# A four-layer block on one core: three single-pass products on high and low parts for the gate and up products, a new order of the turn, and a quarter of a state product on VectorE

## The reference

```
w = spline_reconstruct(control_points)          # gate, up, down: [2048,512], [2048,512], [512,2048]
x = x + (silu(h @ gate.T) * (h @ up.T)) @ down.T       # h = layernorm(x)

dA = jnp.exp(d[..., None] * A)                   # for each step of 512, 512 channels, 16 states
state = state * dA + (d * u)[..., None] * b[:, None, :]
y = jnp.einsum('bdn,bn->bd', state, c)
```

## Time and profile before

| | |
|---|---|
| median of 3 runs | 1876.14 us |
| the profiled execution | 1873.21 us, its span 1871.4 us |
| granted TensorE clock, mean | 0.925 |
| TensorE busy | 1607.1 us (86%) |
| GpSimd busy | 1143.8 us (61%) |
| VectorE busy | 1109.2 us (59%) |
| ScalarE busy | 904.2 us (48%) |
| DMA | 276.31 MB, mean 148 GB/s |

### The profile page before, as it was taken

One profiled execution on the slowest core, in us unless ns is written; L12 is line 12 of the kernel. 1 busy time (PEld: TensorE's weight loads), 2 busy tenths in 40 slices (PEclk: granted clock), 3 DMA queues, 4 the chain that ended last, 5 costly groups with the idle time before them and its releaser, 6 DMA issues. The chain is left out here.

```text
span 1871.4 us, 25251 instructions
## 1 busy us (share of the span) xinstructions
PE 1607.1 (86%) x5972; PEld 993.6 (53%) x5973; DVE 1109.2 (59%) x2007; ACT 904.2 (48%) x1355; POOL 1143.8 (61%) x578
## 2 busy tenths in 40 slices
PE   4888847999999999999999546489999999999996
PEld 2333323444444444444444236368887887788885
DVE  3556675565656565656566555955656556556653
ACT  3344425455555555555555353734544445445442
POOL 0222135887878787878789211256666666667664
PEclk9878868999999999999999765589999999999998
DMA  3221044666767676667566753168888888888875
GB/s 124 79 80 66 15 167 129 165 149 126 171 149 149 126 171 149 149 126 170 128 142 124 190 169 137 39 152 197 187 194 187 194 190 183 194 200 194 193 146 105
DMA packets 88164, 276.31 MB, mean 148 GB/s; under 512 B 12321, under 2 KB 13250, under 8 KB 76338
## 3 DMA queue, kind: packets, MB, share of 16 engines
q0 software_dynamic: 42656, 150.93, 41.4%
q1 hardware_dynamic: 45458, 124.79, 21.5%
HBM read 148.78 MB, written 126.90 MB: 147 GB/s over the span
## 5 line engine op out<-in xcount | busy, mean ns | idle before, releaser
L694 DVE TENSOR_TENSOR_SCAN B_E<-bank,B_E 128x512 f32<-128x512 f32 x256 | 306.2, 1211 | 206.7 <-ACT bank L649 199.2
L737 POOL TENSOR_TENSOR B_E<-B_E,B_Cb 128x2048 f32<-128x2048 f32 x64 | 291.9, 4560 | 110.7 <-DVE B_E L694 110.7
L1572 POOL DMA_INDIRECT out_x<-D_y,D_rows x144 | 263.3, 1829 | 84.7 <-issue 43.7
L731 POOL TENSOR_TENSOR B_E<-B_dtu,B_Bb 128x2048 f32<-128x2048 f32 x64 | 292.2, 4567 | 32.9 <-DMA B_Bb<-bc_d 32.9
L610 PE MATMUL bank<-B_Wd,B_inter 128*128 128x512 f32 x512 | 230.7, 597 | 33.2 <-DVE X L688 32.4
L600 PE MATMUL bank<-hT,B_Wg 128*128 128x512 f32 x512 | 236.5, 606 | 23.6 <-DVE B_inter L683 22.5
L649 ACT ACTIVATE bank<-B_dtv,negA 128x512 f32<-128x512 f32 x256 | 171.8, 687 | 137.8 <-DVE B_E L694 137.0
L600 PE MATMUL bank<-hT,B_Wu 128*128 128x512 f32 x512 | 230.2, 592 | 0.0
L1537 POOL DMA_INDIRECT D_rows<-rows_d,D_source x144 | 150.1, 1042 | 127.6 <-DMA out_x<-D_y,D_rows 63.6
L1351 PE MATMUL bank<-W_gu_hi,D_xT_hi 128*128 x580 | 210.8, 363 | 1.0 <-ACT D_xT_hi L1410 0.9
L1352 PE MATMUL bank<-W_gu_lo,D_xT_hi 128*128 x580 | 196.6, 339 | 0.0
(11 more groups left out here) (270 smaller groups left out, 2821.5 us busy)
## 6 DMA issues: line engine op xcount, KB each, us to landing
y_d<-B_E POOLq DMA_DIRECT2D x64, 1024.0 KB, 8.1
W_raw_gu<-in_wgu SPq DMA_DIRECT2D x64, 384.0 KB, 4.7
B_Bb<-bc_d SPq DMA_DIRECT2D x32, 512.0 KB, 5.4
B_Cb<-bc_d SPq DMA_DIRECT2D x32, 512.0 KB, 3.8
W_raw_d<-in_wd SPq DMA_DIRECT2D x64, 256.0 KB, 4.4
rows_d<-C_row SPq DMA_DIRECT2D x4, 1090.0 KB, 4.8
X<-in_x SPq DMA_DIRECT2D x4, 1024.0 KB, 9.1
dt_d<-A_dtv SPq DMA_DIRECT2D x4, 1024.0 KB, 3.9
```

The source lines that it names most:

```text
L694: v.tensor_tensor_scan(E[:, s % NR, c, :], dA[m % 2][:, :], E[:, s % NR, c, :], 0.0, ALU.mult, ALU.add).then_inc(s_done, 1)
L731: g.tensor_tensor(E[:, s % NR, :, :], dtu[b % 2][:, :, :], spread(Bb[jj % 2][:, s % 2, :]), ALU.mult).then_inc(dbu_done, 1)
L737: g.tensor_tensor(E[:, s % NR, :, :], E[:, s % NR, :, :], spread(Cb[jj % 2][:, s % 2, :]), ALU.mult).then_inc(prod_done, 1)
L1572: g.indirect_dma_start(a["out"], bass.IndirectOffsetOnAxis(ap=rows[i][:, ROW - 1:ROW].bitcast(U32), axis=0), ysb[:, i, :], None, compute_o ...
```

## The change

**Products.** hT and the weights are kept as a high part (rounded to the single-pass format) and a low part (the rest). Every gate and up product becomes three single-pass ones: high by high, high by low, low by high. Tiles of hT get a second instruction on VectorE (`turn_lo`), weight units as well (`unit_lo`); of a gate or up unit the blend is now done in PSUM, before ScalarE's copy. Room for the low parts comes from single buffers for masks and drive input, three row buffers BC of one row each, inter chunks in three buffers with silu in place, and coefficients in DRAM (coef_d), of which one group at a time is loaded.

**Order.** In a turn `gate_up` of chunk 0 comes first, then a unit, the down products, a unit and `gate_up` of chunk 1. On ScalarE and VectorE decays, silus, scans and the rest are interleaved anew.

**Last quarter.** GpSimd's `weigh` covers three quarters and waits for three; VectorE's `weigh_last` does the fourth.

```diff
-            hT = s.enter_context(nc.sbuf_tensor("hT", [P, KC, NB * L], F32))
-            coef = s.enter_context(nc.sbuf_tensor("coef", [NSEL, 3, INTER], F32R))
+            hT_hi, hT_lo = (s.enter_context(nc.sbuf_tensor(f"hT_{h}", [P, KC, NB * L], F32R)) for h in ("hi", "lo"))
+            coef_gu = s.enter_context(nc.sbuf_tensor("coef_gu", [NSEL, 2, GW], F32R))
+            coef_dn = s.enter_context(nc.sbuf_tensor("coef_dn", [NSEL, D], F32R))
             powers = s.enter_context(nc.sbuf_tensor("powers", [NSEL, KC, 2, P], F32R))
...
+            sp.wait_ge(c_lo, 8)
+            sp.dma_start(coef_gu[:, :, :].bitcast(F32), coef[:, 0:2, 0:GW].bitcast(F32)).then_inc(coef_moved, 16)
+            sp.dma_start(coef_d[:, 0:2, :], coef[:, 0:2, :].bitcast(F32)).then_inc(coef_moved, 16)
+            sp.wait_ge(c_lo, 12)
+            sp.dma_start(coef_dn[:, :].bitcast(F32), coef[:, 2, 0:D].bitcast(F32)).then_inc(coef_moved, 16)
+            sp.dma_start(coef_d[:, 2, :], coef[:, 2, :].bitcast(F32)).then_inc(coef_moved, 16)
+            sp.wait_ge(coef_moved, 64)
...
+            def turn_lo(t):
+                v.wait_ge(hT_first, t + 1)
+                v.tensor_tensor(hT_lo[:, :, t * P:(t + 1) * P], bank[t % 2][:, :].rearrange("p (k l) -> p k l", k=KC),
+                                hT_hi[:, :, t * P:(t + 1) * P], ALU.subtract).then_inc(hT_done, 1)
...
                 v.tensor_scalar(xn[:, t % 2, :], X[:, t, :], mv[:, t, 0:1], rstd[:, t:t + 1], ALU.subtract, ALU.mult).then_inc(xn_done, 1)
+                if t >= 1:
+                    turn_lo(t - 1)
+            turn_lo(NT - 1)
...
-                act.activation(hT[:, :, t * P:(t + 1) * P], bank[t % 2][:, :].rearrange("p (k l) -> p k l", k=KC), ACT.Copy).then_inc(hT_done, 1)
-            act.wait_ge(ld_pw, 16)
+                act.activation(hT_hi[:, :, t * P:(t + 1) * P], bank[t % 2][:, :].rearrange("p (k l) -> p k l", k=KC), ACT.Copy).then_inc(hT_first, 1)
...
-        Wg, Wu = [sb(f"Wg{i}", [P, KC, GW]) for i in range(2)], [sb(f"Wu{i}", [P, KC, GW]) for i in range(2)]
+        Wg, Wu = ([[sb(f"W{n}_{h}{i}", [P, KC, GW], F32R) for h in ("hi", "lo")] for i in range(2)] for n in ("g", "u"))
-        words = [sb(f"masks{i}", [P, GW + D // 2], I32) for i in range(2)]
-        msk = [w[:, :].bitcast(U8) for w in words]
-        sil = [sb(f"sil{i}", [P, L]) for i in range(2)]
-        inter = [sb(f"inter{i}", [P, 2, L]) for i in range(2)]
-        dtv, dtu = sb("dtv", [P, KC, L]), [sb(f"dtu{i}", [P, KC, L]) for i in range(2)]
-        Bb, Cb = [sb(f"Bb{i}", [P, 2, L]) for i in range(2)], [sb(f"Cb{i}", [P, 2, L]) for i in range(2)]
-        NR = 4
+        words = sb("masks", [P, GW + D // 2], I32)
+        msk = words[:, :].bitcast(U8)
+        NI, NBC, NR = 3, 3, 4
+        inter = [sb(f"inter{i}", [P, L]) for i in range(NI)]
+        dtv, dtu = sb("dtv", [P, KC, L]), sb("dtu", [P, KC, L])
+        BC = [sb(f"BC{i}", [P, L]) for i in range(NBC)]
         E = sb("E", [P, NR, KC, L])
...
+        def drive_op(s):
+            return s if s < 2 else 2 * s - 1
+        def weigh_op(s):
+            return 2 * s + 2 if s + 2 < STEPS else STEPS + s
...
+            def op_done(op):
+                s, drives = steps[op]
+                sp.wait_ge(dbu_done if drives else prod_done, s + 1)
+                if not drives:
+                    sp.wait_ge(last_done, s + 1)
+            def load_row(op):
+                s, drives = steps[op]
+                if op >= NBC:
+                    op_done(op - NBC)
+                sp.dma_start(BC[op % NBC][:, :], spread(s % NS + (0 if drives else NS), s // NS)).then_inc(ld_bc[op % NBC], 16)
+            steps = {drive_op(s): (s, True) for s in range(STEPS)}
+            steps.update({weigh_op(s): (s, False) for s in range(STEPS)})
+            load_row(0)
             load_dtu(0)
             for c in range(KC):
                 load_dtv(0, c)
-            for b in range(NB):
-                for j in range(NJ):
-                    jj = NJ * b + j
-                    if jj >= 2:
-                        sp.wait_ge(dbu_done, 2 * (jj - 1))
-                    sp.dma_start(Bb[jj % 2][:, :, :].rearrange("p n l -> p (n l)"), spread(0, b, j)).then_inc(ld_b[jj % 2], 16)
...
+            load_masks(0)
+            for op in range(1, 2 * STEPS):
+                load_row(op)
+                s, drives = steps[op - NBC] if op >= NBC else (0, True)
+                b, group = (s + 1) // NS, s // 8 + 1
+                if drives and (s + 1) % NS == 0 and b < NB:
+                    load_dtu(b)
+                if not drives and (s + 2) % NS == 0 and s + 2 < STEPS:
+                    for c in range(KC):
+                        sp.wait_ge(dA_done, (s + 1) * KC + c + 1)
+                        load_dtv((s + 2) // NS, c)
+                if not drives and s % 8 == 0 and group < 2 * NB:
+                    units = NU if s == 0 else unit_job[(s // 2 - 1, 1)][0] + 1
+                    sp.wait_ge(used, units)
+                    sp.dma_start(coef_gu[:, :, :].bitcast(F32), coef_d[:, 0:2, group * GW:(group + 1) * GW]).then_inc(ld_coef, 16)
+                    if group % 2 == 0:
+                        sp.dma_start(coef_dn[:, :].bitcast(F32), coef_d[:, 2, group // 2 * D:(group // 2 + 1) * D]).then_inc(ld_coef, 16)
+                    load_masks(group)
...
-                        mm = pe.matmul(ps[:, :], W[:, k, ch * P:(ch + 1) * P], hT[:, k, tb * L:(tb + 1) * L], start=k == 0, stop=k == KC - 1)
+                        hi, lo = (t[:, k, ch * P:(ch + 1) * P] for t in W)
+                        h_hi, h_lo = (t[:, k, tb * L:(tb + 1) * L] for t in (hT_hi, hT_lo))
+                        pe.matmul(ps[:, :], hi, h_hi, start=k == 0, stop=False)
+                        pe.matmul(ps[:, :], hi, h_lo, start=False, stop=False)
+                        mm = pe.matmul(ps[:, :], lo, h_hi, start=False, stop=k == KC - 1)
...
+                gate_up(jj, 0)
                 if (jj, 0) in unit_job:
                     n, g = unit_job[(jj, 0)]
                     weights(n, unit_of(jj, 0), g)
-                gate_up(jj, 0)
+                if jj:
+                    down(jj - 1)
                 if (jj, 1) in unit_job:
                     n, g = unit_job[(jj, 1)]
                     weights(n, unit_of(jj, 1), g)
-                if jj:
-                    down(jj - 1)
                 gate_up(jj, 1)
...
-            def copy_unit(n, unit, buf):
-                act.wait_ge(a_ps, n + 1)
-                act.activation(w_unit(unit, buf), A_[n % 2][:, :], ACT.Copy).then_inc(a_used, 1)
+            def unit_first(n, unit, buf):
+                if unit < 4:
+                    act.wait_ge(blended, blends_ahead(n) + 1)
+                    act.activation(w_unit(unit, buf, 0), A_[n % 2][:, :], ACT.Copy).then_inc(first_done, 1)
+                else:
+                    act.wait_ge(a_ps, n + 1)
+                    act.activation(Wd[buf][:, unit - 4, :], A_[n % 2][:, :], ACT.Copy).then_inc(first_done, 1)
             def silu(jj, ch):
                 n = chunk_job[(jj, ch)]
                 act.wait_ge(a_ps, n + 1)
-                act.wait_ge(b_used, n - 1)
-                act.activation(sil[n % 2][:, :], A_[n % 2][:, :], ACT.Silu).then_inc(a_used, 1)
+                if 2 * jj + ch >= NI:
+                    act.wait_ge(y_ps, 4 * (jj - 1 + ch))
+                act.activation(chunk(jj, ch)[:, :], A_[n % 2][:, :], ACT.Silu).then_inc(sil_done, 1)
...
+            def unit_and_decay(jj, pos, s, c):
+                if (jj, pos) not in unit_job:
+                    decay(s, c)
+                    return
+                n, g = unit_job[(jj, pos)]
+                unit = unit_of(jj, pos)
+                if unit < 4:
+                    decay(s, c)
+                unit_first(n, unit, g % 2)
+                if unit >= 4:
+                    decay(s, c)
...
+            decay(0, 0)
+            decay(0, 1)
             for jj in range(NB * NJ):
-                for c in range(KC):
-                    decay(2 * jj, c)
-                if (jj, 0) in unit_job:
-                    n, g = unit_job[(jj, 0)]
-                    copy_unit(n, unit_of(jj, 0), g % 2)
+                decay(2 * jj, 2)
+                decay(2 * jj, 3)
                 silu(jj, 0)
-                if (jj, 1) in unit_job:
-                    n, g = unit_job[(jj, 1)]
-                    copy_unit(n, unit_of(jj, 1), g % 2)
-                for c in range(KC):
+                unit_and_decay(jj, 0, 2 * jj + 1, 0)
+                for c in range(1, KC):
                     decay(2 * jj + 1, c)
+                if jj < NB * NJ - 1:
+                    unit_and_decay(jj, 1, 2 * jj + 2, 0)
+                    decay(2 * jj + 2, 1)
                 silu(jj, 1)
...
-                v.wait_ge(a_used, n + 1)
+                m = msk[:, unit % 2 * 2 * GW:(unit % 2 + 1) * 2 * GW] if unit < 4 else msk[:, 4 * GW + (unit - 4) * D:4 * GW + (unit - 3) * D]
+                v.wait_ge(ld_msk, 16 * (g + 1))
```

(64 more changed lines are left out.)

118 lines of the change are left out of this document (58 added, 60 removed).

## The result

The changed kernel takes 1938.08 us (median of four runs, 1935.45 to 1941.49) where the kernel before takes 1875.12 (1872.77 to 1880.24): a ratio of 1.0333, with a 95% interval from 1.0306 to 1.036: slower by 63 us. The forecast was 1770, faster by 5.6%.

A forecast was written before the change was run, and what follows sets the result against it. A ring of waits in the feed-forward/state stage, paced by TensorE, the fullest engine, bounds the kernel. −141 + 11 + 9 + 6 + 7 + 4 = −104 us from 1873.2 gives 1769, stated as 1770; forecast 1745 to 1800 (0.58), wider range 1735 to 1840.

The forecast's parts named there:

- the hold: VectorE's last-quarter product waits only until the running GpSimd product ends; the other bound, none, saves 22 us in all.
- The rule that the forecast weighed: VectorE instruction with two SBUF inputs and GpSimd one reading SBUF exclude each other for a whole instruction; sum follows it.
- 583: First to last weighing: 21 turns of 18.9 us plus 10.5 of 17.7, against 724.1 before, −141 us.
- +11: GpSimd products beside which a held VectorE instruction slips in take longer: 63 × 0.17 us.
- +9: Batch changes: single-buffered drive input reloads, some 3 us stay, three times; bounds 3 and 15 us.
- +6 +7 +4: Before the first weighing: preparation's tiles +6, four coefficient moves +7 (bounds 3 and 12), new stage's start to first weighing +4.
- 18.3: TensorE's need per turn with units, in us, with single-pass products at 0.22; 17.4 without units.
- B: Rival, slower: even step's last quarter misses its window, held to W+7.9 (W: weighing's start), 23.4 us turns, 1912 us; chance 0.09.
- A: Rival, missed windows: odd step's last quarter late, held 4.5 us more; all 14 missing gives 1827 us; chance 0.20.
- C: Rival, no hold: VectorE's last-quarter product passes as the additions do, 1737 us; chance 0.10.
- D: Rival: single-pass gate and up products take as long as full-precision ones, 0.43 us each, over 1900 us; chance 0.01.
- The signs named ahead: Profile signs: 18.9 us turns, last-quarter product about 1.0 to 1.5 us; near 3 means A, turn over 22 B, 0.65 C.

The follow-up runs named there:

- The run with GpSimd's own wait: Changed kernel, register values masked, GpSimd's next drive waiting for the end of GpSimd's own weighing: 1816.48 us, ratio 0.9715.
- the control: Changed kernel with only three register values (expert numbers) masked in the last stage, an edit every further variant carries: 1945.28 us, ratio 1.038.
- the product from PSUM: Changed kernel, values masked, fourth scan written to PSUM so VectorE's last-quarter product reads one input there: 1780.03 us, ratio 0.952.
- The floor without the last quarter: Changed kernel, values masked, last quarter weighed by neither engine, GpSimd's transfer waiting for all four scans: 1764.54 us.
- the pair of runs that differ in the passes alone: Changed kernel, masked, last-quarter product from PSUM: single-pass gate and up products 1780.03 us, one full-precision product of the high parts 1849.33 us.
- the one-input operation: Changed kernel, masked, last-quarter product replaced by VectorE's tensor_scalar on one SBUF tensor and two scalars: 1987.35 us, unreadable as a total; stage 738.0 against 758.6.

## Why the prediction was wrong

**The step that failed is the hold.** The forecast took from four normalizations that "VectorE waited for the end of the running GpSimd instruction, then got in before or beside the following one", and wrote "I take the hold, until the running GpSimd product ends". It is so in 33 of 64 cases. In 16 the product arrived in time and was passed over, and in 12 it came after the weighing's end. Instead of about 1.0 to 1.5 us it lasts 4.12. The row that the forecast read the earlier trace rows was read rightly, and did not hold the case. Its 14.08 us are three held normalizations and one that was not (0.53 us), between these products of GpSimd and that of 261.39:

```profile
256.83 4.60 POOL L437 TENSOR_TENSOR B_Rgate<-B_Rgate,B_table 128x2048 f32<-128x2048 f32 x1 [18.35 <-DMA B_select<-in_select]
257.37 4.34 DVE L445 TENSOR_SCALAR B_xn<-X,B_mv,B_rstd 128x512 f32<-128x512 f32 x1 [0.30 <-PE bank L458]
261.64 4.72 DVE L445 TENSOR_SCALAR B_xn<-X,B_mv,B_rstd 128x512 f32<-128x512 f32 x1
266.04 4.68 POOL L437 TENSOR_TENSOR B_Rdown<-B_Rdown,B_table 128x2048 f32<-128x2048 f32 x1
266.28 4.72 DVE L445 TENSOR_SCALAR B_xn<-X,B_mv,B_rstd 128x512 f32<-128x512 f32 x1
```

Each held one ended 0.28 to 0.29 us after the product that ran, the first two with the next product directly behind. So VectorE was let in at every boundary there; but no product stood directly behind a transfer issue, as 26 of the 64 weighings of the changed kernel do. What failed is the step from three normalizations to 64 products beside another sequence of GpSimd instructions.

The run with GpSimd's own wait is the kernel with the forecast's hold, let in at the end of every weighing for which the product is in time. It has 628.8 us from first to last weighing against 758.6 of the control: the boundaries at which VectorE was passed over, or came late because of it, cost 130 us.

The rule that the forecast weighed (the Trainium skill, "SBUF — State Buffer", Who interferes with whom) says that whichever of the two comes first holds the other off for the whole instruction. That the two exclude each other agrees with the traces here, and it spoke against the change. How long the waiting one can stay shut out does not follow from it: here it was up to four instructions of GpSimd, and 12.4 us.

**The sum, term by term.** From first to last weighing the forecast had 583 + 11 + 9 = 603 us; measured are 758.2, 155 more. Some 130 of these are the missed boundaries. The other 26 are seen in the run with GpSimd's own wait: its turns without a reload take 19.3 us on average, where 583 + 11 over 31.5 turns is 18.9, and its three turns with a reload 26.3 to 26.4, so 21 us more for the three where **+9** was forecast, with a bound of 15. The mean of its held products is 2.4 us and not 1.0 to 1.5, so even a hold to the next boundary was priced too low. With the product from PSUM, which has no hold and no slip-in, the stage takes 594.1 us: 18.2 a turn, and 24.9, 25.2 and 26.1 for the three with a reload. The forecast without a hold had 22 us less than 583, 17.8 a turn, so the rest of the turn was about right. The **+11** for drives beside a slip-in came true in kind (4.96 to 5.08 us instead of the 4.5 of before where VectorE got in, about three times the 0.17 taken).
The start: **+6 +7 +4** put the first weighing at 330 us. It came at 338.2, 8 us later. The stage begins 20.1 us later (TensorE's first unit at 311.77) instead of 13: VectorE's last subtraction of the preparation ends at 301.87 where it was 291.32, 10.5 us later and not 6, and the time from there to the stage grew by 9.6 us where the moves were put at 7 (they are 2.75 MB, not 2.65). The way from the stage's start to the first weighing is 5 longer instead of 4. The last coefficient write (768 KB) is issued at 302.6 us and takes 8.8 us to land, just ahead of the new stage; that it sets the start was not tried apart. What stands behind the last weighing grew by 2.4 us. 1769 + 155 + 8 + 2 gives 1934, and the profiled execution took 1935.

**TensorE, GpSimd.** Single-pass products start 0.227 us apart, inside the bounds of 0.215 and 0.24 but above the 0.22 taken: 0.3 us a turn. The weighing is 3.42 us at the least and 3.50 in the median, as said. The floor without the last quarter, 18.6 us a turn with TensorE busy 98% of it, lies near the 18.3 that the forecast gave TensorE.

**The rivals.** B, slower, had the price nearly right (a hold to W+7.9, 23.4 us a turn, 1912 us; measured W+8.4 to 8.8 in the even steps that were passed over, 24.1 us, 1938) and the even step as its place, but not the trigger: the product there came in time and was passed over. A, the odd step that comes late, happens too, in eight odd steps, each held 4.8 us, near the 4.5 it said. I gave B 0.09 because I counted the margin to an arrival, 0.5 us, and took for certain that an arrival in time is enough. C, no hold, is excluded by the 4.12 us; D by the pair of runs that differ in the passes alone, 1780 and 1849 us.

The signs named ahead served: a mean near 3 us was to show A and a turn over 22 B, and L783 with 4.12 and the weighings with 24.07 show that the forecast's turn had not come.

**Still open.** Why the 28 products whose weighing had begun after a pause were let in, although the drive's record starts 0.02 to 0.05 us ahead of the weighing's end there too (0.32 to 0.37 us in 12 of the 16, 0.04 to 0.06 in the other four), and the 16 were not. The pause in front of the weighing parts them without exception, in the control's 44 too, and for the one-input operation in all but two of 50, which came within 0.05 us of the weighing's end; a wait behind the weighing removes the case. What GpSimd does in between isn't visible in the trace, and a kernel in which only the pause in front of the weighing is changed was not run. That the one-input operation is held because of the mode in which it runs was not tried apart from its operands.

## What to carry to other kernels

Before moving a product to VectorE beside a GpSimd that reads SBUF in long instructions, look at what it reads: with one input in PSUM it ran at 0.68 us whatever GpSimd did, from SBUF alone it cost 3.4 to 4.1 us on average and made VectorE the bound. When such an operation can't be avoided, price a missed boundary at the length of all GpSimd products that are queued, and try a break between two of them (a wait for its own result took 129 us out of this kernel). When two changes relieve two engines, time them together too: here the move alone gave 5 us and the cut in passes alone 25, and each gave 44 us more once the other was in.

## What the runs showed that was not expected

- Between two products that GpSimd runs back to back VectorE is not always let in: it was in 28 of 44 cases, and in 16 it was passed over, all with the first of the two directly behind a transfer issue. Holds last up to 12.4 us, over four instructions. With a wait for GpSimd's own result between the two, a pause of 0.08 us in the records, it was let in in 48 of 48.
- VectorE's `tensor_scalar` on one SBUF tensor is held as long as a product of two; once let in it ends 0.28 to 0.29 us after GpSimd's instruction, the product 0.54 to 0.57 us after.
- A drive beside which VectorE's product got in has a record of 4.94 to 5.08 us, with the one-input operation 4.69 to 4.81. In the kernel before, without either, drives take 4.49 to 4.54 us or, a few of them, 4.80 to 4.83.
- Masking three register values in the last stage makes what follows the last weighing 845.7 us instead of 836.8.
